# Gate bias as columns in tanh and silu, the first product moved into the next block, square roots two groups behind

## The chip, the cores and the metric

The kernel runs on one core of a Trainium2 chip. The metric is the device time of one execution in microseconds (us), the median of several runs.

## The reference

Two transformer-like layers over x of 4 x 512 x 128, fp32. What the change touches is in the second one: an attention whose pair features go through a square root, and eight experts, all of them computed for all tokens.

```python
# second layer: x, xn = layernorm(x), per batch of 512 tokens
e = relu(sqrt(relu(q_i + k_j) + 1e-8) - sqrt(relu(-q_i - k_j) + 1e-8))  # i, j tokens; 64 channels
scores = e @ Wphi
ex = exp(scores - max)
out_attn = (ex @ V + (sum_j ex * e) @ We + ...) / sum(ex)

x1 = xn @ w1[e] + b1[e]; x2 = xn @ w2[e] + b2[e]      # 128 -> 256
z = x1 * x2
s = silu(z @ wg[e] + bg[e])                            # 256 -> 256
y = s @ w3[e] + b3[e]
out = sum over e of share[e] * y
```

## The kernel before

The first layer and the routing take the first 460 us or so. The second layer (`second_layer`) works in 32 **blocks** m of 64 query tokens, two blocks to a loop body (`tile`, a hardware loop over 16 tiles with the first and last written out). Block m also does the expert m % 8 for the batch m // 8.

One block has 8 **groups** gg of 4 slots c; a slot is one pair of query tokens, a 128x512 fp32 tile `feat` in `arena`. Positions are written (gg, c). Every engine has its own program, in an order written by hand:

- VectorE runs `reduce_pair` (L1021) in each slot: feature tile times the broadcast softmax row in PSUM, with a sum. Between slots stand, by the `work` table, `product` (z, L1047), `silu` (L1053), `finish`, `add_experts` (L1064), `largest` (the row maximum `nmax` and the `shift`, L1013 and L1015, at (4,3)), `split` (L1073, at (7,1)) and one or two relu features a group (L1007) for the block after next.
- TensorE runs `broadcast` (L1295) in each slot, at most three banks ahead of VectorE: it waits for `reduced`. Between them come `scores` (L1282, eight calls a block, at the places of `SCORES_AT`; each waits for `e_ready`), the expert's `left_product` (L1331), `right_product` (L1339), `gate` (L1347 for the bias, L1348 for the weights), `down` (L1361), and transposes.
- ScalarE makes one or two relu features a group (L1149), one group behind VectorE, and after each second group one **square root** over eight tiles (L1157, 128x4096); in group 5 `exponentials` for the next block (L1166, L1169) and `tanh_half` (L1193); `keep_left` (L1185) and `keep_exT` (L1175). Exp and tanh share one activation table, the square root has another.
- GpSimd makes one relu feature a group in two passes (L1258, L1264) and `place` (L1240).
- SyncE loads each expert's weights, and in its gate load the 256 biases as one row (L1436).

The gate bias is added by TensorE: `ones` (1 element) repeated 512 times against a row of `bg`, ahead of the weights. Silu is u * (1 + tanh(u/2)) with the factor 0.5 in `share`. ScalarE's tanh and VectorE's product both read the gate's sum u in PSUM, bank psZ for half 0 and psX for half 1. psX also holds `right_product`, so that one has to wait for the second silu (`s_ready`).

```python
def gate(m, f, half):
    ...
    if half == 0:
        pe.matmul((psZ, psX)[f], bg[0:1, f * P:(f + 1) * P], ones[0:1, 0:1].to_broadcast([1, N]), start=True, stop=False)
```

Ahead of block 0 a prologue makes the features of blocks 0 and 1 (16 groups, all on VectorE), their square roots on ScalarE, the scores of block 0, and the transposed shares for the bias b3 (`shareT`), which VectorE copies after the eighth group (L1113) before it halves `share` (L1115).

Of the kernel before, what the change touches and what calls it, by code (L numbers as in the profile page):

```python
# [22 lines left out]
P = 128  # L23
# [77 lines left out]
def layers_kernel(nc, x, wqk, wv, gate0_w, gate0_b, w1, b1, w2, b2,  # L101
# [7 lines left out]
    with ExitStack() as ctx:  # L109
# [20 lines left out]
        g.bge, g.ones = sb("bge", [1, DFF]), sb("ones_row", [1, 1])  # L130
# [214 lines left out]
def first_layer(nc, g, take):  # L345
# [12 lines left out]
    with ExitStack() as ctx:  # L358
# [65 lines left out]
        def _(sp):  # L424
# [10 lines left out]
            sp.wait_ge(small_in, 16 * len(small))  # L435
# [291 lines left out]
def prepare_constants(pool, g, made, prep):  # L727
# [9 lines left out]
    pool.memset(g.ones[:], 1.0)  # L737
# [156 lines left out]
def second_layer(nc, g, sb):  # L894
# [24 lines left out]
    with ExitStack() as ctx:  # L919
# [6 lines left out]
        b1, b2, bg, ones = g.b1e, g.b2e, g.bge, g.ones  # L926
# [32 lines left out]
        act_passed = sem("act_passed")  # L959
        negq_ready, pool_cut, pool_feat = sem("negq_ready"), sem("pool_cut"), sem("pool_feat")  # L960
# [6 lines left out]
        FEATURE_LAG = 1  # L967
# [25 lines left out]
        SPLIT_AT, SILU_AT = (7, 1), ((6, 2), (6, 3))  # L993
# [6 lines left out]
        with nc.Block() as block:  # L1000
            @block.vector
            def _(dve):
# [134 lines left out]
            def _(act):  # L1137
                def roots(m, j, gg, ahead=False):

                    b, pair0 = slot_parts(m)  # L1140
                    if ahead:
                        if gg % 2:
                            act.wait_ge(feat_ready, m * PAIRS + QUADS * (gg + 1))
                    else:
                        act.wait_ge(reduced, m * PAIRS - 2 * PAIRS + QUADS * (gg + 1))

                        act.sem_inc(act_passed, 1)
                        for c in range(ON_DVE[gg] + ON_POOL[gg], QUADS):
                            act.activation(feat[:, j, QUADS * gg + c, :], kT[:, bass.ds(b * N, N)], ACT.Relu,  # L1149
                                           bias=q2[:, bass.ds(pair0 + GROUPS * c + gg, 1)]).then_inc(act_feat, 1)  # L1150
                        if gg % 2:
                            act.wait_ge(feat_ready, m * sum(ON_DVE) + FEATURES_AHEAD + sum(ON_DVE[:gg + 1]))
                            act.wait_ge(act_feat, (m - 2) * sum(ON_ACT) + sum(ON_ACT[:gg + 1]))
                            act.wait_ge(pool_feat, (m - 2) * sum(ON_POOL) + sum(ON_POOL[:gg + 1]))
                    if gg % 2:
                        grp = feat[:, j, QUADS * (gg - 1):QUADS * (gg + 1), :].rearrange("p k n -> p (k n)")
                        act.activation(grp, grp, ACT.Sqrt, bias=eps[:]).then_inc(e_ready, 2)  # L1157
# [29 lines left out]
                def tanh_half(m, first=False):  # L1187

                    if not first:
                        act.wait_ge(y_done, m)  # L1190
                    for f in range(GT):
                        act.wait_ge(gate_done, m * GT + f + 1)
                        act.activation(s[:, f, :], (psZ, psX)[f], ACT.Tanh, scale=0.5).then_inc(tanh_ready, 1)  # L1193

                def tile(t, first=False, last=False):
                    for j in range(2):
                        m = t * 2 + j
                        none = first and j == 0
                        for gg in range(GROUPS):
# [27 lines left out]
            def _(pool):  # L1227
                def place(m):
# [47 lines left out]
            def _(pe):  # L1276
# [65 lines left out]
                def gate(m, f, half):  # L1342
                    if half == 0 and f == 0:
                        pe.wait_ge(z_ready, (m + 1) * GT)
                        pe.wait_ge(wg_in, (m + 1) * 32)
# [20 lines left out]
                def tile(t, first=False, last=False):  # L1366
                    for j in range(2):
# [15 lines left out]
                            (7, 1): lambda: final or right_product(m + 1, 0),  # L1383
# [44 lines left out]
            def _(sp):  # L1428
# [79 lines left out]
```

## Time and profile before

| | |
|---|---|
| median of 3 runs | 1540.93 us (1539.06 to 1542.65) |
| the profiled execution's own time | 1545.48 us |
| its span | 1543.5 us |
| busy over the span: PE, DVE, ACT, POOL | 86%, 87%, 76%, 27% |
| granted TensorE clock, mean | 0.97 of full speed |
| first reduction of block 0 | at 503.67 us |
| from one block to the next, steady | 32.52 us |

The profile shows one execution. PE is TensorE, PEld its weight loads, DVE VectorE, ACT ScalarE, POOL GpSimd, SP SyncE. The time of the profiled execution is 4.55 us over the median of the runs; sums below are made against it. A line number is that of the kernel before unless said otherwise. "Idle" in brackets is the engine's idle time just before the row, with the work that ended it.

### The profile page before, as it was taken

Reading aid. Unit: us, or ns where it says so; the run is one execution under the profiler, and the core shown is the slowest. Engines: PE = TensorE matmul, PEld = TensorE weight load, DVE = VectorE, ACT = ScalarE, POOL = GpSimd, SP = SyncE. Lnnn points to the kernel's source line nnn. Section 1 sums busy time; section 2 is a strip of 40 time slices with the busy share of each in tenths; the row PEclk is TensorE's granted clock in tenths of the full one; section 3 lists DMA queues with packets and bytes.
Section 4 is the critical chain, followed back from the end, with each engine's and each line's share of the span. In section 5 each row is a group of like instructions: output and inputs, shape, how many; then the busy total and the mean of one; then the engine's idle time right before and its main releaser. Section 6 shows DMA issues by size and latency. Waiting matters only on the chain.

```text
span 1543.5 us, 25266 instructions
## 1 busy us (share of the span) xinstructions
PE 1320.4 (86%) x6313; PEld 598.8 (39%) x6313; DVE 1341.9 (87%) x3714; ACT 1176.4 (76%) x1354; POOL 414.6 (27%) x623
## 2 busy tenths in 40 slices
PE   3798687878775999989999899999999998999997
PEld 2466455555552233333333333333333333333333
DVE  4686687878758899999999999999999999999988
ACT  1566576777626988888888888888888888888860
POOL 1702100000000333333333334333333433333310
PEclk9899899999967999999999999999999999999999
DMA  5001200000000000000000000000000000000001
GB/s 176 14 1 35 13 1 0 0 0 0 0 1 18 14 18 26 20 24 17 17 17 27 24 17 17 17 27 18 23 17 17 20 24 24 17 17 17 27 24 31
DMA packets 36761, 31.59 MB, mean 20 GB/s; under 512 B 4102, under 2 KB 33593, under 8 KB 36722
## 3 DMA queue, kind: packets, MB, share of 16 engines
q1 hardware_dynamic: 35698, 29.79, 6.3%
q0 software_dynamic: 1024, 1.35, 0.8%
q8 instruction: 16, 0.26, 0.1%
q14 instruction: 23, 0.19, 0.0%
HBM read 29.12 MB, written 2.75 MB: 21 GB/s over the span
## 4 chain that ended last, share of the span: by engine, by line
PE 38%; DVE 21%; issue 8%; DVEq 2%; ACT 1%; ACTq 0%
PE ps L1282 12%; DVE arena L1021 10%; PE ps L1295 10%; DVE arena L1007 6%; PE ps L1361 4%; PE ps L1348 3%; PE ps L1331 3%; PE ps L1347 2%; PE ps L1339 2%; DVE z L1047 1%; DVE spread L1073 1%; DVE nmax L1013 1%; PE ps L1303 1%; DVEq L1064 1%; DVEq L1020 1%
## 5 line engine op out<-in xcount | busy, mean ns | idle before, releaser
L1021 DVE SCALAR_TENSOR_TENSOR arena<-arena,ps 128x512 f32<-128x512 f32 x1024 | 676.4, 680 | 62.0 <-PE ps L1295 60.7
L1157 ACT ACTIVATE arena<-arena,eps 128x4096 f32<-128x4096 f32 x128 | 474.5, 3711 | 42.1 <-DVE arena L1007 29.7
L1295 PE MATMUL ps<-spread,sel 128*128 128x512 f16 x1024 | 355.9, 384 | 77.1 <-DVE arena L1021 68.3
L1258 POOL TENSOR_SCALAR arena<-kT,negq 128x512 f32<-128x512 f32 x240 | 170.5, 710 | 533.8 <-DVE arena L1021 530.8
L1149 ACT ACTIVATE arena<-kT,q 128x512 f32 (+1 forms) x360 | 239.4, 719 | 67.4 <-DVE arena L1021 67.4
L1282 PE MATMUL ps<-arena,phi_cols 128*32 128x512 f32 x2048 | 276.0, 613 | 7.5 <-ACT arena L1157 7.5
L1295 PEld LDWEIGHTS ps<-spread,sel 128*128 128x128 f16 x1024 | 96.7, 97 | 452.6 <-DVE arena L1021 365.7
L1007 DVE TENSOR_SCALAR arena<-kT,q 128x512 f32 (+1 forms) x424 | 219.5, 529 | 0.3 <-PEq L760 0.3
L1264 POOL TENSOR_SCALAR arena<-arena,q 128x512 f32<-128x512 f32 x240 | 175.2, 730 | 23.2
L486 ACT ACTIVATE kT<-ps,region 128x512 f32<-128x512 f32 x128 | 88.0, 688 | 106.3 <-DVE region L556 100.2
L1348 PE MATMUL ps<-z,wge 128*128 128x512 f32 x256 | 137.4, 618 | 0.0
L556 DVE TENSOR_REDUCE region<-ps 128x1 f32<-128x512 f32 x128 | 88.0, 688 | 50.0 <-PE ps L658 34.2
L676 PE MATMUL ps<-ident,kT 128*128 128x128 f32 x512 | 80.6, 281 | 47.6 <-DVE pT_lo L572 46.5
L676 PEld LDWEIGHTS ps<-ident,kT 128*128 128x128 f32 x512 | 59.9, 143 | 96.5 <-DVE kT L564 64.8
L1282 PEld LDWEIGHTS ps<-arena,phi_cols 128*32 128x32 f32 x2048 | 41.2, 109 | 129.0 <-issue 111.9
L572 DVE TENSOR_TENSOR pT_lo<-ps,pT_hi 128x512 fp32r<-128x512 f32 x128 | 87.7, 685 | 4.0 <-ACT pT_hi L501 3.2
L657 PE MATMUL ps<-k_hi,q_parts 128*128 128x512 f32 x128 | 66.7, 521 | 24.3 <-DVE k_lo L542 19.3
L1339 PE MATMUL ps<-xnT,w2e 128*128 (+1 forms) x128 | 72.8, 651 | 15.2 <-DVE z L1047 8.4
L1250 POOL TENSOR_SCALAR negq<-q 128x256 f32<-128x256 f32 x4 | 3.5, 870 | 302.9 <-POOLq L760 302.9
L1021 DVE DVE_READ_ACCUMULATOR arena<-arena,ps 128x1 f32 x1024 | 83.5, 82 | 0.0
L501 ACT ACTIVATE pT_hi<-ps 128x512 fp32r<-128x512 f32 x128 | 75.8, 593 | 9.0 <-issue 4.9
L1347 PE MATMUL ps<-ones_row,bge 1*128 1x512 f32 x128 | 71.8, 641 | 0.3 <-DVE z L1047 0.3
(197 smaller groups left out, 1833.8 us busy)
## 6 DMA issues: line engine op xcount, KB each, us to landing
wge<-in_e_wg SPq DMA_DIRECT2D x32, 256.0 KB
w1e<-in_e_w SPq DMA_DIRECT2D x32, 128.0 KB, 2.1
w2e<-in_e_w SPq DMA_DIRECT2D x32, 128.0 KB, 2.1
w3e<-in_e_w SPq DMA_DIRECT2D x32, 128.0 KB, 2.1
region<-in_w SPq DMA_DIRECT2D x1, 2048.0 KB
out<-x SPq DMA_DIRECT2D x4, 256.0 KB, 2.8
region<-in_wqk SPq DMA_DIRECT2D x1, 512.0 KB, 5.1
region<-in_wv SPq DMA_DIRECT2D x1, 512.0 KB, 5.7
```

The costliest lines, as they stand in the source:

```text
L676: ins = pe.transpose(ps[:, TBK[late % 2], m * P:(m + 1) * P], ex[:, late % 4, m * P:(m + 1) * P], g.ident[:])
L1007: dve.tensor_scalar(feat[:, j, QUADS * gg + c, :], kT[:, bass.ds(b * N, N)], q2[:, bass.ds(pair0 + GROUPS * c + gg, 1)], 0.0, ALU.add, ALU ...
L1021: dve.scalar_tensor_tensor(feat[:, j, k, :], feat[:, j, k, :], 1.0, psB[:, k % BANKS, :], ALU.mult, ALU.mult, accum_out=sums[:, j, gg, c:c ...
L1149: act.activation(feat[:, j, QUADS * gg + c, :], kT[:, bass.ds(b * N, N)], ACT.Relu, bias=q2[:, bass.ds(pair0 + GROUPS * c + gg, 1)]).then_ ...
L1157: act.activation(grp, grp, ACT.Sqrt, bias=eps[:]).then_inc(e_ready, 2)
L1258: pool.tensor_scalar(feat[:, j, QUADS * gg + c, :], kT[:, b * N:(b + 1) * N], HUGE, negq[:, b % 2, at - b * N // 2:at - b * N // 2 + 1], A ...
L1264: pool.tensor_scalar(f, f, 1.0, q2[:, at:at + 1], ALU.mult, ALU.add).then_inc(pool_feat, 1)
L1282: ins = pe.matmul(psS[32 * c:32 * (c + 1), :], phi_cols[:, gg, :], feat[:, j, QUADS * gg + c, :], start=(gg == 0), stop=(gg == GROUPS - 1))
L1295: pe.matmul(psB[:, k % BANKS, :], sel[:, gg, c, :], spread[:, j, :], start=True, stop=True).then_inc(bc_done, 1)
L1339: pe.matmul(psX, w2[:, f * P:(f + 1) * P], xnT[:, bass.ds(m // E * N, N)], start=True, stop=True).then_inc(right_done, 1)
L1347: pe.matmul((psZ, psX)[f], bg[0:1, f * P:(f + 1) * P], ones[0:1, 0:1].to_broadcast([1, N]), start=True, stop=False)
L1348: ins = pe.matmul((psZ, psX)[f], wg[:, half * DFF + f * P:half * DFF + (f + 1) * P], z[:, half, :], start=False, stop=(half == 1))
```

## The change

The bias of the gate leaves TensorE. It is loaded once, in the first layer, as columns `bge` (128 x 2 x 8) by two element-wise DMAs; VectorE makes a halved copy `bgh` in the prologue. Tanh takes `bgh` as its bias. GpSimd then adds one to the tanh (`lift`, L1260 after), ahead of its group-6 feature, and silu becomes (u + bg) * lifted, and waits for `lifted`. The silus move from (6,2) and (6,3) to (7,0) and (7,2). `right_product(m + 1, 0)` at (7,1) becomes `right_product(m, 0)` at (0,2) of the next block. `roots` is split: relu features stay one group behind, square roots run two groups behind.

```diff
-            sp.wait_ge(small_in, 16 * len(small))
+            for f in range(GT):
+                sp.dma_start(g.bge[:, f, :], g.e_bg[:, f * P:(f + 1) * P].rearrange("e p -> p e"),
+                             allow_slow_non_contiguous=True).then_inc(small_in, 16)
+            sp.wait_ge(small_in, 16 * (len(small) + GT))
...
-        FEATURE_LAG = 1
+        FEATURE_LAG, ROOT_LAG = 1, 2
...
-        SPLIT_AT, SILU_AT = (7, 1), ((6, 2), (6, 3))
+        SPLIT_AT, SILU_AT, LIFT_AT = (7, 1), ((7, 0), (7, 2)), 6
...
                 def silu(m, f):
-                    dve.wait_ge(tanh_ready, m * GT + f + 1)
-                    dve.scalar_tensor_tensor(s[:, f, :], s[:, f, :], 1.0, (psZ, psX)[f], ALU.add,
-                                             ALU.mult).then_inc(s_ready, 1)
+                    dve.wait_ge(lifted, m * GT + f + 1)
+                    dve.scalar_tensor_tensor(s[:, f, :], (psZ, psX)[f], bg[:, f, bass.ds(m % E, 1)], s[:, f, :],
+                                             ALU.add, ALU.mult).then_inc(s_ready, 1)
...
                         dve.tensor_scalar(share, share, 0.5, None, ALU.mult).then_inc(halved, 1)
+                        dve.tensor_scalar(bgh[:], bg[:], 0.5, None, ALU.mult).then_inc(bg_halved, 1)
...
                         act.wait_ge(gate_done, m * GT + f + 1)
-                        act.activation(s[:, f, :], (psZ, psX)[f], ACT.Tanh, scale=0.5).then_inc(tanh_ready, 1)
+                        act.sem_inc(act_passed, 1)
+                        act.activation(s[:, f, :], (psZ, psX)[f], ACT.Tanh, bias=bgh[:, f, bass.ds(m % E, 1)],
+                                       scale=0.5).then_inc(tanh_ready, 1)
...
                             if gg == 5:
                                 tanh_half(m, none)
+                            late = behind(m, j, gg, ROOT_LAG)
+                            if late[2] % 2 and makes(late, first, last):
+                                roots(*late[0:3])
                             late = behind(m, j, gg, FEATURE_LAG)
                             if makes(late, first, last):
-                                roots(*late[0:3])
-
+                                features(*late[0:3])
+
+                act.wait_ge(bg_halved, 1)
                 for n in range(2 * GROUPS):
-                    roots(n // GROUPS, n // GROUPS, n % GROUPS, ahead=True)
+                    if n % 2:
+                        roots(n // GROUPS, n // GROUPS, n % GROUPS, ahead=True)
...
+                def lift(m):
+
+                    if m:
+                        pool.wait_ge(placed, 2 * m)
+                    for f in range(GT):
+                        pool.wait_ge(tanh_ready, m * GT + f + 1)
+                        pool.tensor_scalar(s[:, f, :], s[:, f, :], 1.0, 1.0, ALU.mult, ALU.add).then_inc(lifted, 1)
...
-                    if half == 0:
-                        pe.matmul((psZ, psX)[f], bg[0:1, f * P:(f + 1) * P], ones[0:1, 0:1].to_broadcast([1, N]), start=True, stop=False)
                     ins = pe.matmul((psZ, psX)[f], wg[:, half * DFF + f * P:half * DFF + (f + 1) * P], z[:, half, :],
-                                    start=False, stop=(half == 1))
+                                    start=(half == 0), stop=(half == 1))
...
-                            (7, 1): lambda: final or right_product(m + 1, 0),
+                            (0, 2): lambda: none or right_product(m, 0),
...
-                    sp.dma_start(bg[:], g.e_bg[bass.ds(e, 1), :]).then_inc(wg_in, 16)
```

The order of instructions at three places follows; in each, the names are those of the sections above.

ScalarE in the loop body from the square root of groups 2 and 3 to the features of group 4, before:

```order
L1157 ACTIVATE arena<-arena,eps 128x4096 [waits pool_feat]
L1166 ACT_TABLE_LOAD [waits spread_ready,exT_done]
L1166 ACTIVATE ex<-ps,shift 128x512 [waits shift_ready]
L1169 ACTIVATE exh<-ps,shift 128x512 [waits spread_ready]
L1192 REGISTER_ALU [waits y_done]
L1193 ACTIVATE s<-ps 128x512 [waits gate_done] x2
L1145 REGISTER_ALU
L1149 ISA [waits reduced]
L1149 ACTIVATE arena<-kT,q 128x512
```

and in the changed kernel, from the exponentials to the square root of groups 2 and 3, with what follows it:

```order
L1170 ACT_TABLE_LOAD [waits spread_ready,exT_done]
L1170 ACTIVATE ex<-ps,shift 128x512 [waits shift_ready]
L1173 ACTIVATE exh<-ps,shift 128x512 [waits spread_ready]
L1196 REGISTER_ALU [waits y_done]
L1198 ISA [waits gate_done]
L1198 ACTIVATE s<-ps,bgh 128x512
L1198 REGISTER_ALU [waits gate_done]
L1198 ACTIVATE s<-ps,bgh 128x512
L1157 REGISTER_ALU
L1158 REGISTER_ALU [waits feat_ready]
L1159 REGISTER_ALU [waits act_feat]
L1161 ACT_TABLE_LOAD [waits pool_feat]
```

The square root of groups 2 and 3 stood ahead of the exponentials and now stands behind the tanhs; likewise that of groups 4 and 5 now follows `keep_left` and `keep_exT` instead of preceding them. In both the table load stands ahead of the wait for `shift_ready`.

TensorE at (0,1) and (0,2), before (broadcast, broadcast, scores) and, behind it, in the changed kernel (L1317 is the broadcast, L1361 the right product, L1304 the scores):

```order
L1295 MATMUL ps<-spread,sel 128x512 [waits reduced]
L1294 REGISTER_ALU
L1295 MATMUL ps<-spread,sel 128x512 [waits reduced]
L1278 REGISTER_ALU
L1282 MATMUL ps<-arena,phi_cols 32x512 [waits e_ready]
```

```order
L1317 MATMUL ps<-spread,sel 128x512 [waits reduced]
L1316 REGISTER_ALU
L1317 MATMUL ps<-spread,sel 128x512 [waits reduced]
L1361 MATMUL ps<-xnT,w2e 128x512 [waits s_ready]
L1300 REGISTER_ALU
L1304 MATMUL ps<-arena,phi_cols 32x512 [waits e_ready]
```

The right product now stands between the broadcast of (0,2) and the fifth call of `scores`.

ScalarE at the start of the second layer, before and, behind it, in the changed kernel:

```order
L1136 UNCONDITIONAL_BRANCH [waits barrier_Pool_Activation_PE_DVE_SP_release]
L1157 ACT_TABLE_LOAD [waits feat_ready]
L1157 ACTIVATE arena<-arena,eps 128x4096
L1157 ACTIVATE arena<-arena,eps 128x4096 [waits feat_ready] x3
L1166 ACT_TABLE_LOAD
```

```order
L1140 UNCONDITIONAL_BRANCH [waits barrier_Pool_Activation_PE_DVE_SP_release]
L1161 ACT_TABLE_LOAD [waits feat_ready,bg_halved]
L1161 ACTIVATE arena<-arena,eps 128x4096
L1161 ACTIVATE arena<-arena,eps 128x4096 [waits feat_ready] x3
L1170 ACT_TABLE_LOAD
```

The first square root now also waits for the halved bias, which VectorE makes behind `share`.

## Rows read from the trace of the kernel before

**Rows 1.** Busy time by engine, 700 to 1500 us: PE, PEld, DVE, ACT, POOL, clock, DMA.

```profile
700.00:1500.00 800.00, 734.85 (x3603) 270.43 (x3596) 752.95 (x2208) 694.88 (x608) 292.46 (x439) 1.00 0.07 20
```

**Rows 2.** Waits of VectorE, 700 to 1500 us: total us, times, longest.

```profile
DVE arena L1021 <- PE ps L1295: 45.1, 102, 1.6
```

**Rows 3.** Timeline, VectorE, groups 3 and 4: start, us, engine, line, tile, count, [idle].

```profile
1007.45 0.68 DVE L1021 SCALAR_TENSOR_TENSOR arena<-arena,ps 128x512 f32<-128x512 f32 x1
...
1009.07 0.69 DVE L1021 SCALAR_TENSOR_TENSOR arena<-arena,ps 128x512 f32<-128x512 f32 x1 [0.93 <-PE ps L1295]
...
1012.88 0.15 DVE L1015 TENSOR_SCALAR shift<-nmax 128x1 f32<-128x1 f32 x1
```

**Rows 4.** Timeline, TensorE, the gate bias of half 0.

```profile
1006.64 1.12 PE L1347 MATMUL ps<-ones_row,bge 1*128 1x512 f32 x2
```

**Rows 5.** Timeline, VectorE, group 6 to the next block.

```profile
1020.40 0.69 DVE L1053 SCALAR_TENSOR_TENSOR s<-s,ps 128x512 f32<-128x512 f32 x1
...
1021.61 0.73 DVE L1007 TENSOR_SCALAR arena<-kT,q 128x512 f32 x1
...
1023.53 0.47 DVE L1007 TENSOR_SCALAR arena<-kT,q 128x512 f32 x1
...
1024.53 0.08 DVE L1021 DVE_READ_ACCUMULATOR arena<-arena,ps 128x1 f32 x1
...
1027.95 0.69 DVE L1021 SCALAR_TENSOR_TENSOR arena<-arena,ps 128x512 f32<-128x512 f32 x1 [0.23 <-PE ps L1295]
```

**Rows 6.** Timeline, TensorE, the same stretch.

```profile
1021.15 1.12 PE L1339 MATMUL ps<-xnT,w2e 128*128 x2 [0.18 <-DVE s L1053]
...
1024.67 0.39 PE L1295 MATMUL ps<-spread,sel 128*128 128x512 f16 x1 [0.86 <-DVE arena L1021]
1024.99 1.07 PE L1282 MATMUL ps<-arena,phi_cols 128*32 128x512 f32 x8
...
1026.52 1.06 PE L1282 MATMUL ps<-arena,phi_cols 128*32 128x512 f32 x8
```

**Rows 7.** Timeline, ScalarE, one block.

```profile
1010.67 3.71 ACT L1157 ACTIVATE arena<-arena,eps 128x4096 f32<-128x4096 f32 x1 [1.00 <-DVE arena L1007]
1014.40 1.28 ACT L1166 ACT_TABLE_LOAD   x1
1015.70 0.69 ACT L1166 ACTIVATE ex<-ps,shift 128x512 f32<-128x512 f32 x1
...
1017.81 1.96 ACT L1149 ACTIVATE arena<-kT,q 128x512 f32 x3
...
1021.22 3.71 ACT L1157 ACTIVATE arena<-arena,eps 128x4096 f32<-128x4096 f32 x1
1024.83 0.67 ACT L1185 ACTIVATE left<-ps,b1e 128x512 f32<-128x512 f32 x1
...
1025.67 1.94 ACT L1149 ACTIVATE arena<-kT,q 128x512 f32 x3
```

**Rows 8.** Groups by line, 700 to 1500 us: count | busy us, mean ns | idle.

```profile
L1047 DVE SCALAR_TENSOR_TENSOR z<-ps,b2e,left 128x512 f32<-128x512 f32 x50 | 37.2, 744 | 0.0
...
L1185 ACT ACTIVATE left<-ps,b1e 128x512 f32<-128x512 f32 x50 | 33.4, 668 | 0.0
...
L1193 ACT ACTIVATE s<-ps 128x512 f32<-128x512 f32 x48 | 26.1, 604 | 0.0
```

**Rows 9.** Timeline, ScalarE, start of the second layer.

```profile
468.01 1.28 ACT L1157 ACT_TABLE_LOAD   x1 [5.00 <-DVE arena L1007]
...
490.45 0.69 ACT L1166 ACTIVATE ex<-ps,shift 128x512 f32<-128x512 f32 x1 [5.32 <-DVE shift L1015]
```

**Rows 10.** Timeline, VectorE, start of the second layer.

```profile
479.75 0.20 DVE L1115 TENSOR_SCALAR share<-share 128x128 f32<-128x128 f32 x1
```

**Rows 11.** Timeline, GpSimd, one block.

```profile
1021.38 0.69 POOL L1264 TENSOR_SCALAR arena<-arena,q 128x512 f32<-128x512 f32 x1
```

**Rows 12.** Timeline, VectorE, last block.

```profile
1526.46 0.69 DVE L1021 SCALAR_TENSOR_TENSOR arena<-arena,ps 128x512 f32<-128x512 f32 x1 [1.05 <-PE ps L1295]
```

More of the change, by code:

```diff
@@ L129, in layers_kernel @@
         g.b1e, g.b2e, g.b3 = sb("b1e", [P, GT, E]), sb("b2e", [P, GT, E]), sb("b3", [E, D])
-        g.bge, g.ones = sb("bge", [1, DFF]), sb("ones_row", [1, 1])
+        g.bge, g.bgh = sb("bge", [P, GT, E]), sb("bgh", [P, GT, E])
         g.w1e, g.w2e = sb("w1e", [P, DFF]), sb("w2e", [P, DFF])
@@ L736, in prepare_constants @@
     pool.memset(g.eps[:], EPS_RHO)
-    pool.memset(g.ones[:], 1.0)
     pool.memset(g.rho, -math.sqrt(EPS_RHO))
@@ L925, in second_layer @@
         phi_cols, eps = g.phi_cols, g.eps
-        b1, b2, bg, ones = g.b1e, g.b2e, g.bge, g.ones
+        b1, b2, bg, bgh = g.b1e, g.b2e, g.bge, g.bgh
         ex = sb("ex2", [P, 2, N])
@@ L959, in second_layer @@
         act_passed = sem("act_passed")
+        lifted, bg_halved = sem("lifted"), sem("bg_halved")
         negq_ready, pool_cut, pool_feat = sem("negq_ready"), sem("pool_cut"), sem("pool_feat")
-        FEATURE_LAG = 1
+        FEATURE_LAG, ROOT_LAG = 1, 2
         SCORES_AT = {(6, 2): 0, (7, 0): 1, (7, 2): 2, (0, 0): 3, (0, 2): 4, (1, 0): 5, (2, 2): 6, (3, 2): 7}
@@ L1137, in _, with features @@
             def _(act):
+                def features(m, j, gg):
+                    b, pair0 = slot_parts(m)
+                    act.wait_ge(reduced, m * PAIRS - 2 * PAIRS + QUADS * (gg + 1))
+                    act.sem_inc(act_passed, 1)
+                    for c in range(ON_DVE[gg] + ON_POOL[gg], QUADS):
+                        act.activation(feat[:, j, QUADS * gg + c, :], kT[:, bass.ds(b * N, N)], ACT.Relu,
+                                       bias=q2[:, bass.ds(pair0 + GROUPS * c + gg, 1)]).then_inc(act_feat, 1)
@@ L1138, in roots @@
                 def roots(m, j, gg, ahead=False):
-                    b, pair0 = slot_parts(m)
                     if ahead:
-                        if gg % 2:
-                            act.wait_ge(feat_ready, m * PAIRS + QUADS * (gg + 1))
-                    else:
[L1145 to L1154, printed above, removed]
@@ L1155, in roots @@
-                    if gg % 2:
-                        grp = feat[:, j, QUADS * (gg - 1):QUADS * (gg + 1), :].rearrange("p k n -> p (k n)")
-                        act.activation(grp, grp, ACT.Sqrt, bias=eps[:]).then_inc(e_ready, 2)
+                        act.wait_ge(feat_ready, m * PAIRS + QUADS * (gg + 1))
+                    else:
+                        act.wait_ge(feat_ready, m * sum(ON_DVE) + FEATURES_AHEAD + sum(ON_DVE[:gg + 1]))
+                        act.wait_ge(act_feat, (m - 2) * sum(ON_ACT) + sum(ON_ACT[:gg + 1]))
+                        act.wait_ge(pool_feat, (m - 2) * sum(ON_POOL) + sum(ON_POOL[:gg + 1]))
@@ L1159, in exponentials @@
+                    grp = feat[:, j, QUADS * (gg - 1):QUADS * (gg + 1), :].rearrange("p k n -> p (k n)")
+                    act.activation(grp, grp, ACT.Sqrt, bias=eps[:]).then_inc(e_ready, 2)
                 def exponentials(m, j, before=2):
@@ L1192, in tanh_half @@
                         act.wait_ge(gate_done, m * GT + f + 1)
-                        act.activation(s[:, f, :], (psZ, psX)[f], ACT.Tanh, scale=0.5).then_inc(tanh_ready, 1)
+                        act.sem_inc(act_passed, 1)
+                        act.activation(s[:, f, :], (psZ, psX)[f], ACT.Tanh, bias=bgh[:, f, bass.ds(m % E, 1)],
+                                       scale=0.5).then_inc(tanh_ready, 1)
                 def tile(t, first=False, last=False):
@@ L1237, in place @@
                             pool.wait_ge(placed, 2 * m + h)
+                        pool.wait_ge(lifted, (m + 1) * GT)
                         made = min(m * sum(ON_POOL) + sum(ON_POOL[:-1]), (MB - 2) * sum(ON_POOL))
@@ L1267, in _ @@
                     for gg in range(GROUPS):
+                        if gg == LIFT_AT:
+                            lift(m)
+                        if gg == GROUPS - 1 and m + 2 < MB:
+                            place(m)
                         if m + 2 < MB:
-                            if gg == GROUPS - 1:
-                                place(m)
                             features(m + 2, gg)
@@ L1344, in gate @@
                         pe.wait_ge(z_ready, (m + 1) * GT)
[L1345 to L1347 removed]
+                        pe.wait_ge(wg_in, (m + 1) * 16)
                     ins = pe.matmul((psZ, psX)[f], wg[:, half * DFF + f * P:half * DFF + (f + 1) * P], z[:, half, :],
[L1349 removed]
+                                    start=(half == 0), stop=(half == 1))
                     if half:
```

## The prediction

> **What bounds the kernel now.** First the busy times of a long steady stretch [rows 1]: VectorE works 752.95 of 800 us (94%), TensorE 734.85, ScalarE 694.88, GpSimd 292.46. VectorE is nearest to full, so next its waits [rows 2]: in these 24.6 blocks (800 / 32.52) it idles 102 times for broadcasts, 45.1 us, four times and 1.83 us a block, and for nothing else. So a block is VectorE's work, some 30.7 us, plus waits for TensorE's queue. Where they stand is read from the timeline. The largest is at (4,0): reductions normally start 0.61 us apart, this one 1.62 after the last (1007.45 to 1009.07), 1.01 too late [rows 3]. Ahead of its broadcast TensorE had the bias matmul of gate half 0 and two passes of weights [rows 4]. The others are small and stand at (0,1), (0,3) and (1,0), where scores and `left_product` crowd TensorE; the one at (0,3) ends at 1027.95 [rows 5].
>
> The frame for what follows is S, the end of `shift` (1012.88 + 0.15 = 1013.03) [rows 3]. From it ScalarE runs exponentials and tanh. TensorE starts the scores that need the square root of groups 4 and 5 at T = 1026.52 = S + 13.49 [rows 6]. VectorE's (0,3) follows T by 1.43 [rows 5, 6], and the rest of the lap back to the next S hangs on that. T and the wait at (4,0) set the lap of 32.52.
>
> **The change, part by part.**
>
> *Bias matmuls gone.* Two a block, 1.12 us for a pair of passes, 1.05 of it not overlapped [rows 4]. The one at (3,3) frees 1.05 us just where VectorE came 1.01 too late; VectorE then runs from its own queue: -1.01 a block. The one at (4,3) lies where TensorE waits for VectorE anyway: 0.
>
> *Silu.* It gets a per-partition operand. `product` with one takes 0.744 us [rows 8] against silu's 0.69 [rows 5]: +0.06 each. Both stand ahead of (7,3). But the second silu moves behind (7,2), so the reduction that frees the bank for (0,0) ends at 1024.61 (S + 11.58) less 0.60 plus 0.06: S + 11.04 [rows 5].
>
> *Right product at (0,2).* It leaves a place where TensorE had time (0: the wait for (7,2) came behind it) and enters one where it has none. Broadcast (0,0) comes 0.06 after the bank is free, scores 0.32 later, and from there to the scores at (0,2) it was 1.53 [rows 6]: S + 12.95. The product itself lasts 1.12, some 0.2 of it beside its neighbours [rows 6], an estimate of 0.9. TensorE is ready for those scores at S + 13.85.
>
> *Square roots later.* They now follow the exponentials. Count ScalarE from S: the exp can start 0.04 after the shift (490.41 to 490.45), its table load being done before [rows 9]. In the block shown the load came later only because a square root ended at 1014.38. From the exp's start to the features behind the tanhs it is 2.11 (1015.70 to 1017.81); the bias operand makes a tanh longer, bounded by the plain 604 ns and the 668 of `keep_left`, which has one: +0.13 for two; the table load and its switch 1.30; the square root 3.61 to its successor; three features 1.84; `keep_left` and `exT` 0.84; the square root of groups 4 and 5 3.71 [rows 7, 8]. With some 0.2 for the end of the last tanh the sum is 13.78, and `scores` may start at about S + 13.8. In the old order this root was done 1.6 us before T (1021.22 + 3.71 = 1024.93). So both chains, TensorE's and ScalarE's, arrive together, and T goes from S + 13.49 to S + 13.85: **+0.36**.
>
> The Trainium skill ("ScalarE: Activation LUTs", section "What ACT_TABLE_LOAD costs") gives about 93 ns for each pointer operand; by that the two tanhs cost 0.06 more than by the rows, 1.7 us over the kernel.
>
> *GpSimd's two passes.* One lasts 0.69 [rows 11], GpSimd is busy a third of the time, and tanh is done near S + 2.6, the feature of group 5 near S + 5.6. The lifts end near S + 7.2, silu wants the first at S + 7.4: no wait. They push the feature of group 6 back by some 0.2. Today VectorE's feature at (7,0) lasts 0.73 instead of 0.47, ending 0.27 after GpSimd's pass (1022.07) [rows 5, 11]. The new meeting is a coin toss: 0.26 won or 0.27 lost. Taken at 0 here; the loss is a rival.
>
> *Steady sum:* -1.01 + 0.36 = **-0.65 a block**, a lap of 31.87. For 29 blocks -18.9 us.
>
> *Ends.* Block 0 is held by TensorE around both bias matmuls: -2.1 (twice 1.05). In the last tile VectorE waits for the gates too, once 1.05 [rows 12]: -2 for two blocks. At the very end `down` needs the second silu, now three reductions of 0.61 later, part of it slack: between 0 and +1.8, taken at +0.9. Together -3.2.
>
> *The prologue.* ScalarE's first square root starts at 468.01 [rows 9], as soon as two groups of features are there. Now it waits for `bg_halved`, which VectorE makes behind eight groups, the copies and the halving of `share`, 479.75 [rows 10]. It comes near 480.05: +12.05. What is behind is serial: four roots, the last scores, the row maximum, the exp at 490.45, the split, the first broadcast. VectorE waited for that maximum already, and its work behind it was packed. So **+12.05** is paid in full. Bounds: 0 if something hides it, +14 if TensorE also slows in the longer gap.
>
> *Other edits.* The two column loads go out in the first layer, 1024 elements each, hundreds of us ahead of any reader: 0. One load fewer an expert: 0, since no engine waits for weights.
>
> **Sum:** -18.9 - 3.2 + 12.05 = **-10.0 us**: 1545.5 - 10.0 = 1535.5 for the profiled execution, and, as that is 4.55 over the median, **1531 us** against 1540.9. A measurement of this kernel can tell some 0.2% (3.1 us) from no change.
>
> **The rivals.**
>
> 1. *The lift costs VectorE its feature at (7,0).* GpSimd wins the coin toss, the feature ends 0.27 later than today, T is S + 14.12, the lap 32.14. +0.27 x 29 = +7.8: 1539. For it: the old collision [rows 5, 11], and GpSimd's passes now follow one another closely; against it: my offsets put VectorE's start some 0.05 ahead. The Trainium skill ("SBUF — State Buffer", section "Who interferes with whom") says that these two engines share a pair of ports, that whoever issues first holds it for its whole instruction and the other blocks. The trace agrees, with 0.73 against 0.47.
>
> 2. *ScalarE's chain becomes the bound: slower than before.* Place: from S through tanh and two square roots to `scores` at (0,2). The forecast has the chain at 13.8 and it repeats each block, so every 0.1 us costs 2.9. The gain of all else is used up when T passes S + 14.2, 0.4 above. Five instructions in it have waits that they did not have there, and an own wait cost 0.16 ahead of the root at 1019.92 to 1021.22 (features end 1019.77 = 1017.81 + 1.96, load 1.30 before the root) [rows 7]. At 0.16 each T is S + 14.6, the lap 32.6, the sum +2.3 - 3.2 + 12.05 = +11: 1552. For it: no slack. Against it: the waits in question are for things long done.
>
> 3. *The table switch drains the engine.* The exp's load starts 0.02 after the root before it ended (1010.67 + 3.71 to 1014.40) and the exp 1.30 later [rows 7]: no drain. If there were one of 1.38 behind tanh, T would be S + 15.2, the lap 33.2 and the kernel +28: 1569. The same section of "ScalarE: Activation LUTs" in the Trainium skill counts such a drain, 1380 ns on top of 1283 for the load; the trace shows the second figure and not the first.
>
> 4. *The prologue's wait is hidden.* Then the sum is -22: 1519. It needs VectorE to have later slack there, and I see none.
>
> 5. *The lap drops more.* If ScalarE's chain is shorter by the 0.2 allowed for tanh's end and VectorE wins the toss, T is S + 13.6, the lap 31.6, -7.3: 1524.
>
> **How the numbers follow.** Forecast 0.50; rival 1 0.17; rival 2 0.15; rival 3 0.02; rival 4 0.08; rival 5 0.08. Predicted is the forecast's 1531. The range 1519 to 1545 takes in rivals 1, 4 and 5 and the near part of 2; outside stay the far part of 2 and rival 3. Faster by over 0.2% (below 1537.8): forecast 0.46, half of rival 1, rivals 4 and 5: 0.71. Within 0.2%: a tail of the forecast, most of the other half of rival 1, a little of 2: 0.16. Slower: the rest of 2, and 3: 0.13.
>
> **What would show it.** Right: first square root of the second layer near 480 instead of 469, first reduction near 515.7 instead of 503.67; no wait at (4,0); one wait of about 1 us at (0,3) in place of the small ones; ScalarE idle about 1 us ahead of the exp, none ahead of the roots behind it; block to block 31.9. Wrong: TensorE idle for `e_ready` by more than 0.2 at (0,2) (rival 2); a feature at (7,0) of 0.9 or more (rival 1); a gap between tanh and table load (rival 3); a first reduction near 504 (rival 4).

## The result, and the profile after

The changed kernel takes 1547.64 us (median of 10 runs, 1543.43 to 1552.29) against 1541.72 us for the kernel before (10 runs, 1536.67 to 1545.58). The ratio is 1.0038 with a 95% interval of 1.0020 to 1.0056: slower by some 6 us. The forecast was 1531 us, with 1545 as the upper end of its range.

The prediction's own signs come first. The start of the second layer, ScalarE and then VectorE (timeline; columns as in [rows 3]):

```profile
476.93 1.28 ACT L1161 ACT_TABLE_LOAD   x1 [17.08 <-DVE bgh L1119]
...
497.72 0.69 ACT L1170 ACTIVATE ex<-ps,shift 128x512 f32<-128x512 f32 x1 [3.68 <-DVE shift L1018]
```

```profile
461.15 13.11 DVE L1010 TENSOR_SCALAR arena<-kT,q 128x512 f32<-128x512 f32 x32 [0.32 <-PEq L762]
...
476.70 0.15 DVE L1119 TENSOR_SCALAR bgh<-bge 128x16 f32<-128x16 f32 x1
...
496.80 0.69 DVE L1016 TENSOR_REDUCE nmax<-ps 128x1 f32<-128x512 f32 x1 [16.78 <-PE ps L1304]
```

The same two points on VectorE in the kernel before:

```profile
464.32 13.11 DVE L1007 TENSOR_SCALAR arena<-kT,q 128x512 f32<-128x512 f32 x32 [0.32 <-PEq L760]
...
489.53 0.69 DVE L1013 TENSOR_REDUCE nmax<-ps 128x1 f32<-128x512 f32 x1 [6.42 <-PE ps L1282]
```

ScalarE now idles 17.08 us until VectorE has written `bgh`. From VectorE's first feature to the row maximum it was 25.21 us before (464.32 to 489.53); now it is 35.65 (461.15 to 496.80).

One block in the loop, VectorE from the shift to its two waits:

```profile
1017.07 0.15 DVE L1018 TENSOR_SCALAR shift<-nmax 128x1 f32<-128x1 f32 x1
...
1025.26 0.69 DVE L1010 TENSOR_SCALAR arena<-kT,q 128x512 f32 x1
...
1032.46 0.69 DVE L1024 SCALAR_TENSOR_TENSOR arena<-arena,ps 128x512 f32<-128x512 f32 x1 [0.76 <-PE ps L1317]
...
1033.54 0.69 DVE L1024 SCALAR_TENSOR_TENSOR arena<-arena,ps 128x512 f32<-128x512 f32 x1 [0.38 <-PE ps L1317]
```

The same block on ScalarE and TensorE, against [rows 7] and [rows 6]:

```profile
1014.90 1.28 ACT L1170 ACT_TABLE_LOAD   x1
1017.25 0.69 ACT L1170 ACTIVATE ex<-ps,shift 128x512 f32<-128x512 f32 x1 [1.07 <-DVE shift L1018]
...
1018.41 1.27 ACT L1198 ACTIVATE s<-ps,bgh 128x512 f32<-128x512 f32 x2
1019.70 1.28 ACT L1161 ACT_TABLE_LOAD   x1
1020.99 3.71 ACT L1161 ACTIVATE arena<-arena,eps 128x4096 f32<-128x4096 f32 x1
...
1027.29 3.70 ACT L1161 ACTIVATE arena<-arena,eps 128x4096 f32<-128x4096 f32 x1
```

```profile
1028.28 0.39 PE L1317 MATMUL ps<-spread,sel 128*128 128x512 f16 x1 [1.59 <-DVE arena L1024]
...
1030.04 1.03 PE L1361 MATMUL ps<-xnT,w2e 128*128 x2
1031.04 1.07 PE L1304 MATMUL ps<-arena,phi_cols 128*32 128x512 f32 x8
```

This is the forecast nearly to the digit. The exp's table load is done before the shift. The square root of groups 4 and 5 ends 13.77 us behind the shift's end (1027.29 + 3.70 - 1017.22; forecast 13.78) and the scores at (0,2) start 13.82 behind it (13.85). No wait is left at (4,0); one of 0.76 stands at (0,3), one of 0.38 at (1,0). The feature at (7,0) takes 0.69 in this block, little less than the 0.73 of the kernel before, so here the meeting with GpSimd's passes changed next to nothing; in the block before, it takes 0.48. The two tanhs take 1.27 us instead of 1.09: 0.09 each for the bias operand (693 ns against 604 on average), which is the figure of the Trainium skill cited above and not the 0.064 that I took from `keep_left`.

The block before that one reads otherwise:

```profile
991.12 0.69 DVE L1024 SCALAR_TENSOR_TENSOR arena<-arena,ps 128x512 f32<-128x512 f32 x1 [0.63 <-PE ps L1317]
...
992.42 0.69 DVE L1024 SCALAR_TENSOR_TENSOR arena<-arena,ps 128x512 f32<-128x512 f32 x1 [0.60 <-PE ps L1317]
...
1000.64 0.69 DVE L1024 SCALAR_TENSOR_TENSOR arena<-arena,ps 128x512 f32<-128x512 f32 x1 [0.71 <-PE ps L1317]
...
1001.72 0.69 DVE L1024 SCALAR_TENSOR_TENSOR arena<-arena,ps 128x512 f32<-128x512 f32 x1 [0.38 <-PE ps L1317]
```

VectorE waits here at (6,2) and (6,3), 0.63 and 0.60 us, where no wait stood in the kernel before; the other two are those at (0,3) and (1,0) again. The cause stands on TensorE. Stretches of that lap and of the next, with columns as in [rows 1] (after POOL the granted clock, the DMA share and GB/s):

```profile
984.20:987.40 3.20, 1.13 (x4) 0.39 (x4) 3.20 (x12) 3.11 (x5) 0.72 (x2) 1.00 0.28 82
988.00:991.30 3.30, 3.26 (x12) 0.96 (x12) 2.67 (x11) 3.29 (x1) 2.81 (x4) 0.50 0.00 0
...
1017.00:1020.20 3.20, 1.13 (x5) 0.21 (x3) 3.17 (x12) 2.93 (x5) 0.91 (x2) 1.00 0.24 82
1020.90:1024.00 3.10, 3.06 (x19) 0.90 (x21) 3.10 (x13) 3.09 (x2) 2.81 (x4) 1.00 0.00 0
```

TensorE's granted clock is 1.00 (2.4 GHz) up to 987.4 us and 0.50 (1.2 GHz) from 988 to 991.3. Ahead of the fall the engine was busy 1.13 us of 3.20. In the next lap it was busy 1.13 of 3.20 at the same place, and the clock stayed. The kernel before has the same place at

```profile
980.80:984.00 3.20, 1.95 (x9) 0.79 (x8) 3.20 (x11) 3.17 (x4) 0.50 (x1) 1.00 0.34 82
```

with 1.95 busy. In the changed kernel the scores call after it lasts 1.94 us at the low clock and 1.07 in the next lap:

```profile
988.61 1.94 PE L1304 MATMUL ps<-arena,phi_cols 128*32 128x512 f32 x8
```

```profile
1021.37 1.07 PE L1304 MATMUL ps<-arena,phi_cols 128*32 128x512 f32 x8
```

A lap is the time from one start of the row maximum `nmax` to the next. Laps alternate between 31.84 and 33.02, with a mean of 32.41 over 29 of them (939.92 us), where they were 32.52 (943.18 us). In these 29 the clock falls 14 times. The long stretch of [rows 1] now has a mean clock of 0.97:

```profile
700.00:1500.00 800.00, 699.04 (x3524) 258.67 (x3517) 753.68 (x2217) 701.04 (x613) 328.39 (x489) 0.97 0.07 20
```

TensorE has 35.8 us less work than in [rows 1], VectorE as much as before; VectorE's waits sum to 44.4 us where they were 45.1 [rows 2], only in other places: 77 of them instead of 102.

Where the time went in the profiled executions (1547.3 against 1543.5 us of span):

| piece, by VectorE's rows | before | after | difference | forecast |
|---|---|---|---|---|
| start to the first feature of the second layer (code not changed) | 464.32 | 461.15 | -3.17 | 0 |
| first feature to first row maximum | 25.21 | 35.65 | +10.44 | +12.05 |
| first lap | 34.82 | 33.58 | -1.24 | -2.1 |
| 29 laps | 943.18 | 939.92 | -3.26 | -18.9 |
| last lap and end | 75.97 | 77.00 | +1.03 | -1.1 |

The line that failed is the fourth; the fifth is off by 2.1 us as well. In the last block the clock falls once more, early on, where it was 1.00 before. `right_product` takes 1.91 us there, and VectorE waits 1.26 and 1.33 us where it had no wait:

```profile
1510.30:1517.00 6.70, 5.49 (x9) 2.04 (x10) 4.35 (x13) 0.00 (x0) 0.47 (x2) 0.50 0.01 2
```

```profile
1512.92 1.91 PE L1361 MATMUL ps<-xnT,w2e 128*128 128x512 f32 x2
```

```profile
1515.30 0.69 DVE L1024 SCALAR_TENSOR_TENSOR arena<-arena,ps 128x512 f32<-128x512 f32 x1 [1.26 <-PE ps L1317]
1517.33 0.69 DVE L1024 SCALAR_TENSOR_TENSOR arena<-arena,ps 128x512 f32<-128x512 f32 x1 [1.33 <-PE ps L1317]
```

### The profile page after: what moved, and what is told of

The parts are those of the page before. It is cut to its first block, busy times and chain, and to the rows that moved or that the text cites. A ratio compares the mean times of both kernels' runs of the same rounds, so it can differ in the third digit from the quotient of the medians.

```text
span 1547.3 us, 25187 instructions
## 1 busy us (share of the span) xinstructions
PE 1266.9 (82%) x6185; PEld 580.6 (38%) x6185; DVE 1338.0 (86%) x3715; ACT 1177.0 (76%) x1354; POOL 459.9 (30%) x686
## 2 busy tenths in 40 slices
DMA packets 38777, 31.56 MB, mean 20 GB/s; under 512 B 6150, under 2 KB 35609, under 8 KB 38738
## 4 chain that ended last, share of the span: by engine, by line
PE 34%; DVE 24%; issue 7%; POOL 2%; DVEq 2%; ACT 1%; POOLq 0%; ACTq 0%
DVE arena L1024 13%; PE ps L1304 10%; PE ps L1317 9%; DVE arena L1010 5%; PE ps L1361 4%; PE ps L1381 4%; PE ps L1368 3%; PE ps L1353 3%; DVE z L1050 1%; DVE s L1056 1%; DVE nmax L1016 1%; ACT arena L1161 1%; POOL s L1260 1%; DVE spread L1076 1%; POOL arena L1284 1%
## 5 line engine op out<-in xcount | busy, mean ns | idle before, releaser
L1317 PE MATMUL ps<-spread,sel 128*128 128x512 f16 x1024 | 368.7, 392 | 126.6 <-DVE arena L1024 117.9
L1304 PE MATMUL ps<-arena,phi_cols 128*32 128x512 f32 x2048 | 286.1, 634 | 21.0 <-ACT arena L1161 20.9
L1317 PEld LDWEIGHTS ps<-spread,sel 128*128 128x128 f16 x1024 | 94.7, 97 | 536.8 <-DVE arena L1024 462.5
L1149 ACT ACTIVATE arena<-kT,q 128x512 f32 (+1 forms) x360 | 235.8, 713 | 35.0 <-DVE arena L1024 35.0
L1010 DVE TENSOR_SCALAR arena<-kT,q 128x512 f32 (+1 forms) x424 | 215.9, 521 | 0.3 <-PEq L762 0.3
L1284 POOL TENSOR_SCALAR arena<-arena,q 128x512 f32<-128x512 f32 x240 | 182.8, 762 | 23.4
L1368 PE MATMUL ps<-z,wge 128*128 128x512 f32 x256 | 130.8, 593 | 0.3 <-DVE z L1050 0.3
L1304 PEld LDWEIGHTS ps<-arena,phi_cols 128*32 128x32 f32 x2048 | 41.5, 110 | 148.4 <-issue 101.5
L1189 ACT ACTIVATE left<-ps,b1e 128x512 f32<-128x512 f32 x64 | 43.5, 680 | 54.3 <-PE ps L1353 54.3
L1361 PE MATMUL ps<-xnT,w2e 128*128 (+1 forms) x128 | 70.6, 634 | 8.6 <-DVE z L1050 8.4
```

The source lines that it names most:

```text
L1010: dve.tensor_scalar(feat[:, j, QUADS * gg + c, :], kT[:, bass.ds(b * N, N)], q2[:, bass.ds(pair0 + GROUPS * c + gg, 1)], 0.0, ALU.add, ALU ...
L1284: pool.tensor_scalar(f, f, 1.0, q2[:, at:at + 1], ALU.mult, ALU.add).then_inc(pool_feat, 1)
L1304: ins = pe.matmul(psS[32 * c:32 * (c + 1), :], phi_cols[:, gg, :], feat[:, j, QUADS * gg + c, :], start=(gg == 0), stop=(gg == GROUPS - 1))
L1317: pe.matmul(psB[:, k % BANKS, :], sel[:, gg, c, :], spread[:, j, :], start=True, stop=True).then_inc(bc_done, 1)
L1361: pe.matmul(psX, w2[:, f * P:(f + 1) * P], xnT[:, bass.ds(m // E * N, N)], start=True, stop=True).then_inc(right_done, 1)
```

## The experiments

All other kernels ran on three other chips (e1 to e4, e5 to e8, and e9 to e11), where the kernel before takes 1526.85, 1528.26 and 1527.98 us. The first feature of the second layer comes at 444 to 450 us there, instead of 461 or 464. The laps of the changed code are the same (31.82 and 33.04 in e2). Ratios are to the kernel before on the same chip, and laps are compared across chips. The changed kernel itself was not run on these.

**e1_warm.** Changed kernel plus extra matmuls into a free PSUM bank:

```diff
+                def pad(m, j, none, n=2):
+                    if not none:
+                        pe.wait_ge(fin_ready, m)
+                    for _ in range(n):
+                        pe.matmul(psT, sel[:, 0, 0, :], spread[:, j, :], start=True, stop=True)
...
+                            (5, 2): lambda: pad(m, j, none, 2),
+                            (5, 3): lambda: pad(m, j, none, 2),
+                            (6, 0): lambda: pad(m, j, none, 2),
```

> The changed kernel with six more broadcast-sized matmuls a block (two each at (5,2), (5,3) and (6,0)), whose results nobody reads. Theory A (the freed TensorE time thins the stretch from (5,2) to (6,1), and in every second block the granted clock falls there from 2.4 to 1.2 GHz for about 3 us, which costs that lap 1.18 us): the clock stays at 1.00 in the loop, all laps are 31.84 us instead of 31.84 and 33.02 by turns, and the kernel gains about 29 x 0.59 = 17 us on the changed kernel, some 1530 us against 1547.6. Rival B (the long lap belongs to the second half of the loop body, which holds two blocks, by its branch, its instruction fetch or the lift meeting VectorE's features): the laps stay 31.84 and 33.02 or grow, and the time stays near 1547 us or above.

**e2_prologue.** Changed kernel with ScalarE's wait for `bgh` moved behind the prologue's square roots:

```diff
-                act.wait_ge(bg_halved, 1)
                 for n in range(2 * GROUPS):
...
                         keep_left(0, 1, first=True)
+                act.wait_ge(bg_halved, 1)
                 tile(0, first=True)
```

> The changed kernel with ScalarE's wait for the halved bias moved from ahead of the first square roots to ahead of block 0. If that wait is what delays the first exp by 10.4 us (relative to the start of the features), the first reduction comes 10.4 us earlier and the kernel gains as much: about 1537 us, the loop unchanged. If VectorE or TensorE would have been late anyway, the gain is under 5 us.

**e3_both.** Both edits together.

> Both edits of the two kernels before. If the clock's drop and the prologue's wait are independent and are all that the forecast missed or priced, the gains add: 17 + 10 us on the changed kernel, about 1520 us, some 21 us under the kernel before. If one hides behind the other, it is above 1525 us.

Measured: e1 1518.03 us, ratio 0.9939 (0.9923 to 0.9956); e2 1523.14, 0.9976 (0.9967 to 0.9986); e3 1506.53, 0.9863 (0.9846 to 0.9879). The extra matmuls take 16.6 us off (e2 to e3, forecast 17), the moved wait 11.5 (e1 to e3, forecast 10.4). That the two add up is not measured, for want of the changed kernel on that chip: their sum would put it at 1534.6 us, a ratio of 1.005, and on the first chip its ratio was 1.0038 (1.0020 to 1.0056). With the extra matmuls (e3) the clock reads 1.00 in the loop and the 29 laps are 31.81 to 31.89:

```profile
700.00:1400.00 700.00, 634.45 (x3258) 236.12 (x3256) 673.11 (x1982) 628.90 (x552) 297.14 (x442) 1.00 0.07 21
```

Without them (e2) the laps are 31.82 and 33.04 by turns, as on the first chip. The falls of the clock thus cost 17.2 us: 29 laps take 940.01 us in e2 and 922.80 in e3. Rival B, the loop body of two blocks, falls: e3 has the same body, and its laps are even. Prologue of e3, VectorE:

```profile
448.19 13.11 DVE L1010 TENSOR_SCALAR arena<-kT,q 128x512 f32<-128x512 f32 x32 [0.32 <-PEq L762]
...
473.33 0.69 DVE L1016 TENSOR_REDUCE nmax<-ps 128x1 f32<-128x512 f32 x1 [6.27 <-PE ps L1304]
```

It takes 25.14 us from the first feature to the row maximum, as before the change, against 36.21 in e1.

**e4_nobias.** The kernel before without its bias matmuls. It leaves the gate bias out altogether.

```diff
-                    if half == 0:
-                        pe.matmul((psZ, psX)[f], bg[0:1, f * P:(f + 1) * P], ones[0:1, 0:1].to_broadcast([1, N]), start=True, stop=False)
...
-                                    start=False, stop=(half == 1))
+                                    start=(half == 0), stop=(half == 1))
```

> The kernel before with only the two bias matmuls a block left out; the gate bias is not added. All else stays: silus at (6,2) and (6,3), the right product at (7,1), roots one group behind. Theory A: the wait of 1.01 us at (4,0) goes (lap 31.5), but TensorE's queue is thinner by 1.05 us in the stretch behind (4,3), so whether the clock falls tells if the bias matmuls alone kept it up: with a fall in every second block the mean lap is about 32.1 and the kernel about 1527 us, without it 1510 us. Rival B expects no fall of the clock here, laps all alike.

**e10_nobias_pad.** The same with the six extra matmuls.

> The kernel before without its bias matmuls (the gate bias is not added) and with the six extra matmuls a block. If its uneven laps (31.43 to 32.28) are the clock's doing, all laps are now 31.4 to 31.5 and the kernel gains about 7 us on the one without extra matmuls (ratio 0.978). If they come from something else, the laps stay uneven.

Measured: e4 1499.43 us, 0.9824 (0.9808 to 0.9841), 919.71 us for 29 laps, clock 0.951 over the span. e10: 1491.26 us, 0.9761 (0.9741 to 0.9782), 912.62 us for 29. The first of the 29 is short in both (30.87 and 30.86); the others are 31.48 to 32.28 in e4 and 31.45 to 31.56 in e10. So the bias matmuls did hold the clock up in the kernel before: without them it falls there too, more often than in the changed kernel (17 of the 29 laps instead of 14) but at 0.1 to 0.8 us a time, 7.1 us in all. Both matmuls went together; which of the two held the clock was not tested. And they cost 31 us themselves by the lap, 943.18 less 912.62: from 32.52 to 31.48, that is 1.04 a block, where the prediction had 1.01.

**e5_lag1, e6_right, e7_rightlag1.** From e3. The first moves the square roots back to one group behind, the second the silus and the right product, the third does both.

```diff
-        FEATURE_LAG, ROOT_LAG = 1, 2
+        FEATURE_LAG, ROOT_LAG = 1, 1
...
-                            late = behind(m, j, gg, ROOT_LAG)
-                            if late[2] % 2 and makes(late, first, last):
-                                roots(*late[0:3])
                             late = behind(m, j, gg, FEATURE_LAG)
                             if makes(late, first, last):
                                 features(*late[0:3])
+                            if late[2] % 2 and makes(late, first, last):
+                                roots(*late[0:3])
```

```diff
-        SPLIT_AT, SILU_AT, LIFT_AT = (7, 1), ((7, 0), (7, 2)), 6
+        SPLIT_AT, SILU_AT, LIFT_AT = (7, 1), ((6, 3), (7, 0)), 6
...
-                            (0, 2): lambda: none or right_product(m, 0),
+                            (7, 2): lambda: final or right_product(m + 1, 0),
```

> The kernel with six extra matmuls and the moved wait (laps of 31.81 us), with the square roots one group behind again, everything else as changed. Theory: two chains of equal length set T, the start of the scores at (0,2); the one through ScalarE goes when the roots come earlier, the one through the right product stays. But exp and tanh then wait for a root, 1 us or more later than now, so the lifts come late for the silu at (7,0) and hold VectorE. The lap is 32.2 to 32.3, 12 to 14 us more. Rival: roots two groups behind bring nothing or cost, the lap falls below 31.7.

> The same starting point (laps of 31.81 us), with the silus at (6,3) and (7,0) and the next expert's right product at (7,2) in the old block, roots two groups behind. TensorE is then ready for the scores at (0,2) about 0.9 us sooner. Theory (ScalarE's chain binds as well): those scores now wait for the square root, the lap stays within 0.1 of 31.81 and the time within 3 us. Rival (the right product at (0,2) alone had set the lap): the lap falls by 0.4 or more, 11 us less.

> Both edits: silus at (6,3) and (7,0), right product at (7,2), roots one group behind. If each of the two chains alone held the lap at 31.81, only both edits together shorten it: about 31.4 us a lap, 12 us less than with the six extra matmuls and the moved wait alone, provided that the first lift is there in time for (6,3). If the lifts are late, the lap is 31.8 or more.

| | us | ratio | laps | 29 laps | last row maximum to the end |
|---|---|---|---|---|---|
| e3 | 1506.53 | 0.9863 (0.9846 to 0.9879) | 31.81 | 922.80 | 46.49 |
| e5 | 1506.55 | 0.9857 (0.9841 to 0.9874) | 31.80 | 921.87 | 46.78 |
| e6 | 1502.91 | 0.9836 (0.9820 to 0.9852) | 31.82 | 923.14 | 43.27 |
| e7 | 1489.37 | 0.9746 (0.9730 to 0.9763) | 31.39 | 909.84 | 42.60 |

Each chain alone holds the lap at 31.81; only when both are shorter does it fall. (In e5 and e7 the first of the 29 laps is shorter than the rest, 31.16 and 30.76.) For e5 my expectation of 32.2 was wrong: the later lifts still come in time. TensorE's waits, 700 to 1400 us, name the holder. In e6:

```profile
PE ps L1304 <- ACT arena L1161: 8.3, 22, 0.4
```

0.38 us a lap for the square root, a wait that e5's list does not have:

```profile
PE ps L1316 <- DVE arena L1024: 46.9, 91, 1.3
...
PE ps L1303 <- ACT exh L1173: 5.9, 22, 0.3
```

(L1303 and L1316 are the scores and the broadcast of e5; the 5.9 us are a wait for `exh`, not for a root.) e6 takes 3.6 us less than e3 at equal laps, 3.2 of it behind the last row maximum: 2.1 up to the last reduction, where VectorE's waits of 1.25 and 1.44 shrink to 0.16 and 0.65, and 1.1 behind it, where the second silu and `down` come sooner.

**e8_pad2, e11_pad52.** Changed kernel with the moved wait and two extra matmuls instead of six, at (6,0) and at (5,2).

```diff
+                            (6, 0): lambda: pad(m, j, none, 2),
```

> The changed kernel with the moved wait and only two extra matmuls a block, at (6,0), in place of six. They add 0.43 us of work behind the thinnest stretch. Theory A (the clock falls because that stretch is thin): fewer laps are long than the every second one without extra matmuls, perhaps none; whatever number of laps is long, each is 1.2 us above 31.82, and the time follows from their count. If the six worked by their place ahead of the stretch, at (5,2) and (5,3), the laps alternate as before and the time is that without extra matmuls (1523 us where the kernel before took 1527).

> The changed kernel with the moved wait and two extra matmuls a block at (5,2) instead of (6,0). Theory A with the amount of work deciding: about as good as the two at (6,0), that is 27 of 30 laps near 31.82 and some 1510 us where the kernel before takes 1528. With the place deciding: more long laps than there (three of 30), up to every second one (1523 us).

Measured: e8 1510.23 us, 0.9885 (0.9868 to 0.9901); three of the 29 laps and the last one are long by 1.0 us, 925.86 us for 29. e11 1522.02 us, 0.9959 (0.9945 to 0.9974); laps 31.81 and 33.02 by turns, 939.61 us, as in e2, which has none. A lap of each on TensorE, first e8, then e11 (L1390 are the extra matmuls, L1304 the scores call at (6,1)):

```profile
1015.95 0.39 PE L1317 MATMUL ps<-spread,sel 128*128 128x512 f16 x1 [0.58 <-DVE arena L1024]
1017.21 0.39 PE L1317 MATMUL ps<-spread,sel 128*128 128x512 f16 x1 [0.87 <-DVE arena L1024]
1017.44 0.59 PE L1390 MATMUL ps<-spread,sel 128*128 128x512 f16 x2
1018.21 0.39 PE L1317 MATMUL ps<-spread,sel 128*128 128x512 f16 x1 [0.18 <-DVE arena L1024]
...
1019.40 1.07 PE L1304 MATMUL ps<-arena,phi_cols 128*32 128x512 f32 x8
```

```profile
1023.27 0.59 PE L1390 MATMUL ps<-spread,sel 128*128 128x512 f16 x2
...
1025.27 0.39 PE L1317 MATMUL ps<-spread,sel 128*128 128x512 f16 x1 [0.87 <-DVE arena L1024]
1026.27 0.39 PE L1317 MATMUL ps<-spread,sel 128*128 128x512 f16 x1 [0.61 <-DVE arena L1024]
...
1027.68 1.94 PE L1304 MATMUL ps<-arena,phi_cols 128*32 128x512 f32 x8
```

In e8 they stand 1.96 us ahead of the scores call, between the long waits of 0.58 and 0.87 and a short one, and the call lasts 1.07. In e11 they stand 4.41 ahead, two waits of 0.87 and 0.61 come behind them, and it lasts 1.94. The same two matmuls remove most of the falls at one place and none at the other. Nor does the thinnest stretch tell the two apart: of 3.2 us, TensorE is busy 1.57 in it in both, first e8, then e11:

```profile
1015.10:1018.30 3.20, 1.57 (x7) 0.40 (x6) 3.20 (x11) 3.00 (x5) 0.84 (x2) 1.00 0.24 82
```

```profile
1023.10:1026.30 3.20, 1.57 (x7) 0.37 (x5) 3.17 (x12) 2.94 (x5) 0.90 (x2) 1.00 0.26 82
```

So what counts is not the TensorE work of a lap alone, but also where it stands; why that place and not the other is not settled by these two.

**e9_nopad.** e7 without the extra matmuls.

> The kernel of silus at (6,3) and (7,0), right product at (7,2), roots one group behind and moved wait (laps of 31.39 us with six extra matmuls), without the extra matmuls. Theory A: its stretch from (5,2) to (6,1) is as thin as the changed kernel's, so the clock falls again and some laps are 1.0 to 1.2 us longer; with every second one it takes 15 to 17 us more than with them (ratio to the kernel before about 0.985 instead of 0.9746). If the fuller slots at (7,2) keep the clock up, the time stays within 4 us.

Measured: 1505.64 us, 0.9851 (0.9831 to 0.9871), 16.3 us more than e7. But for the first, the laps are 31.37 to 32.67, 922.69 us for 29, so 12.9 of it stands in those; another 4.0 of the 17.3 between the profiled executions stand ahead of the second layer (first feature at 450.43 us instead of 446.48), where the code is the same. The clock falls in 14 of the 29 laps. A better order alone does not keep the clock up.

## Why the prediction was wrong

*"Bias matmuls gone [...] The one at (4,3) lies where TensorE waits for VectorE anyway: 0."* This is the step that failed: the prediction took the clock to stay where it was and put the freed TensorE time at nothing. That is right for VectorE's queue and wrong for the clock. With this work gone TensorE is busy 1.13 instead of 1.95 us of 3.2 ahead of (6,1), its clock falls to 1.2 GHz in every second lap, and VectorE waits 1.2 us at (6,2) and (6,3). That is 14 times 1.18, some 17 us; e2 against e3 measures 16.6. e4 and e10 show that taking out the two bias matmuls is enough to make the clock fall, in the old order too; they do not show that the one at (4,3) alone does it. A fall costs more in the new order, 1.18 us against 0.4 on average in e4. None of the five rivals had it, though the profile's row of the granted clock was there to ask. The Trainium skill ("TensorE: Matmul & The Clock Gate", section "HAM oscillation — how this bites in real kernels") tells of a kernel in which TensorE waits between bursts and runs each next burst at the low clock. The trace agrees, with a difference: here the engine is never idle for long (the longest wait ahead of the fall is 0.87 us), it is only thinly used.

*"-1.01 + 0.36 = -0.65 a block"*, *lap 31.87*: right, with 31.84 in the undisturbed laps and 31.81 with the extra matmuls. So were its parts: the wait at (4,0) gone, T at S + 13.82, two chains that arrive together (e5, e6, e7).

*"The prologue [...] +12.05"*: right in kind and place, shown by e1, e2 and e3. The first square root did start 12.1 us later, counted from the first feature; at the row maximum 10.4 were left (11.1 to 11.5 between e1 and e3). The difference of 1.6 is nearly all in one call. Before, the last scores call ahead of the row maximum had run at the low clock, 3.34 us for 16 passes:

```profile
486.12 3.34 PE L1282 MATMUL ps<-arena,phi_cols 128*32 128x512 f32 x16
```

Now the same call runs at the high one, 1.92:

```profile
494.81 1.92 PE L1304 MATMUL ps<-arena,phi_cols 128*32 128x512 f32 x16
```

*Ends*: forecast -3.2 in all, measured -0.2. The first lap gave 1.24 instead of 2.1, the last lap 0.99 as forecast. From the last row maximum to the end the forecast had -0.1 and the measurement is +2.0. `down`, taken at +0.9, is not the term that failed: behind the last reduction it is +1.15. It now idles for the second silu:

```profile
1537.95 3.47 PE L1381 MATMUL ps<-w3e,s 128*128 128x128 f32 x16 [2.15 <-DVE s L1056]
```

The rest stands ahead of the last reduction, +0.90 where -1 was forecast. The wait of 1.05 [rows 12] and one of 0.67 are gone, but the two of 1.26 and 1.33 in the low stretch of the clock have come. So here too the clock was taken to stay, but it is another edit that lowers it: e4, which lacks the bias matmuls and keeps `right_product` at (7,1), has no low stretch there.

*Rivals.* 1 did not occur (feature at (7,0) 0.69 or less). 2 had the right chain, but it was not longer than counted. 5 did not occur either: the chain was not shorter. 3 falls: load at 1019.70 directly behind the tanhs' end at 1019.68. 4 falls by the rows of the prologue. With the clock as a sixth rival, 17 us on the forecast's 1531 would have given 1548. That this is the measured 1547.64 is in part luck: in the profiled executions the first layer was 3.2 us shorter and the prologue 1.6 cheaper than forecast, and the two ends 3.0 dearer.

## What to carry to other kernels

Work on TensorE that "lies beside a wait and costs nothing" may be what keeps its clock up. Before such work is taken out, look at the busy time left in the thinnest stretch and at the granted clock there, and price one lap at the low clock as a rival. (The thinnest stretch alone does not decide, as e8 and e11 show.) If the clock falls, a few unused matmuls at the right place bring it back: here two at (6,0) were worth 13 us, the same two at (5,2) one or none. And a constant that a loop needs late should be waited for late: one misplaced wait ahead of the loop cost 10 us. When two chains arrive together, neither can be judged by shortening it alone; e7, both shortened, is the fastest version that computes everything, 2.5% under the kernel before.

## What the runs showed of the hardware

- The clock fell in every second lap, although both laps left TensorE busy 1.13 of 3.20 us at the same place. Why one and not the other was not tested.
- A fall cost 1.18 us of a 32 us lap: the granted clock read 0.50 from 988 to 991.3 us. In the old order without bias matmuls (e4) it cost 0.1 to 0.8.
- Two 128x512 f16 matmuls 1.96 us ahead of the scores call removed most of the falls (3 of 29 laps left, e8); the same two 4.41 us ahead removed none (14 of 29, e11).
- A 128x512 tanh with a per-partition bias takes 0.09 us longer than one without (693 ns against 604).
- GpSimd's 128x512 plus-one takes 615 ns, less than its features' 711 and 762; VectorE's silu with the per-partition operand takes 749 ns against 686 without, which is the 0.06 of the forecast.
